# Head attention of a four-layer graph network: batches unrolled, weighted sums issued in pairs, a ring of six

## The reference

```python
q = (x @ W_q).reshape(Bn, Nn, NUM_HEADS, HEAD_DIM).transpose(0, 2, 1, 3)
...
scores = jnp.einsum('bhnd,bhmd->bhnm', q, k) / np.sqrt(HEAD_DIM).astype(np.float32)
adj = adjacency[None, None, :, :]
scores = jnp.where(adj == 0, -jnp.inf, scores)
attn = jax.nn.softmax(scores, axis=-1)
out = jnp.einsum('bhnm,bhmd->bhnd', attn, v)
```

## Time and profile before

| | us |
|---|---|
| median of 3 runs | 3907.07 |
| lowest and highest | 3902.5, 3911.31 |
| the profiled execution | 3912.55 |
| its span, first to last instruction | 3910.8 |
| first score of the head attention starts | 930.7 |
| its last pair of scores | 2873.0 |
| PE busy in the span | 3535.3 (90%) |
| VectorE busy in the span | 3162.2 (81%) |

### The profile page before, as it was taken

One profiled execution on the slowest core, in us unless ns is written; L12 is line 12 of the kernel. 1 busy time (PEld: TensorE's weight loads), 2 busy tenths in 40 slices (PEclk: granted clock), 3 DMA queues, 4 the chain that ended last, 5 costly groups with the idle time before them and its releaser, 6 DMA issues. The chain is left out here.

```text
span 3910.8 us, 71249 instructions
## 1 busy us (share of the span) xinstructions
PE 3535.3 (90%) x21228; PEld 1849.5 (47%) x21228; DVE 3162.2 (81%) x7145; ACT 1732.2 (44%) x3560; POOL 1820.8 (47%) x854
## 2 busy tenths in 40 slices
PE   5669999666999999999999999999968799789999
PEld 4669999441111111111111111111116599689999
DVE  6768888658999989999898998989967555367777
ACT  7811111552656656566565665656625423311100
POOL 2300000113888878888888887888843101100000
PEclk8779999886999999999999999999977799899999
DMA  6422121462100110001101010100125534221211
GB/s 238 168 100 82 50 87 50 154 232 104 27 19 14 29 27 27 21 12 29 27 27 26 8 27 27 27 23 11 28 90 210 199 144 155 101 91 68 82 65 45
DMA packets 66868, 288.66 MB, mean 74 GB/s; under 512 B 12483, under 2 KB 14917, under 8 KB 47045
## 3 DMA queue, kind: packets, MB, share of 16 engines
q1 hardware_dynamic: 64228, 267.55, 19.5%
q0 software_dynamic: 2304, 16.84, 1.0%
HBM read 174.12 MB, written 110.23 MB: 73 GB/s over the span
## 5 line engine op out<-in xcount | busy, mean ns | idle before, releaser
L1327 POOL TENSOR_TENSOR a_w<-a_w,keep_mask_t 128x1024 f32<-128x1024 f32 x768 | 1635.7, 2155 | 407.2 <-ACT a_w L1314 407.1
L1263 DVE CUSTOM_DVE_ANT_0 a_mx_ps<-a_mx_ps,a_mbias 128x512 f32<-128x512 f32 x2112 | 1389.4, 719 | 142.1 <-PE a_mx_ps L1189 129.6
L1314 ACT ACTIVATE a_w<-a_sc_ps 128x512 f32<-128x512 f32 x2048 | 1111.4, 595 | 812.3 <-PE a_sc_ps L1231 810.9
L1205 PE MATMUL a_o_ps<-a_w,a_v 128*33 128x512 f32 x4096 | 1083.6, 609 | 5.7 <-POOL a_w L1327 5.7
L839 PE MATMUL g_acc<-g_hv,g_w 128*128 128x129 f32 x8192 | 924.5, 276 | 36.4 <-ACT g_hv L797 24.8
L839 PEld LDWEIGHTS g_acc<-g_hv,g_w 128*128 128x128 f32 x8192 | 923.1, 193 | 38.1 <-DVE g_w L776 38.1
L776 DVE SCALAR_TENSOR_TENSOR g_w<-g_row,keep_s,keep_mask_t 128x1024 f32<-128x1024 f32 x512 | 647.2, 1282 | 203.7 <-PE g_acc L839 184.4
L1231 PE MATMUL a_sc_ps<-a_qs,a_ks 97*128 97x512 f16 x2048 | 634.4, 392 | 0.0
L1189 PEld LDWEIGHTS a_mx_ps<-a_ks,a_qs 32*128 32x128 f16 x2112 | 94.8, 91 | 893.9 <-DVE a_mx L1263 469.3
L1189 PE MATMUL a_mx_ps<-a_ks,a_qs 32*128 32x512 f16 x2112 | 411.3, 396 | 77.5 <-DVE a_mx L1263 33.4
L1276 DVE TENSOR_TENSOR a_w<-a_w,keep_mask_t 128x1024 f32<-128x1024 f32 x256 | 460.2, 1798 | 0.7
(11 more groups left out here) (178 smaller groups left out, 2278.2 us busy)
## 6 DMA issues: line engine op xcount, KB each, us to landing
p_x<-x SPq DMA_DIRECT2D x24, 1024.0 KB, 8.3
g_h<-h_nodes SPq DMA_DIRECT2D x16, 1032.0 KB, 6.2
p_adj_in<-in_adj SPq DMA_DIRECT2D x16, 1024.0 KB, 7.8
g_row<-u_rows SPq DMA_DIRECT2D x32, 512.0 KB, 7.3
a_v<-v SPq DMA_DIRECT2D x18, 528.0 KB, 3.6
a_ks<-k_hi SPq DMA_DIRECT2D x72, 128.0 KB, 2.8
a_qs<-q_hi SPq DMA_DIRECT2D x72, 128.0 KB, 3.0
v<-p_v SPq DMA_DIRECT2D x8, 1056.0 KB, 6.8
```

The source lines that it names most:

```text
L1205: mm = nc.tensor.matmul(o_ps[2 * HD * a:2 * HD * a + HD + 1, c % 2, :], v[u][:, jt, a, :], w[:, g % PB, a, :], start=(jt == 0), stop=(jt = ...
L1263: last = nc.vector.tensor_tensor_reduce(out=mx_ps[:, buf, a, :], in0=mx_ps[:, buf, a, :], in1=mbias[:, t, kc * BANK:(kc + 1) * BANK], scal ...
L1314: nc.scalar.activation(w[:, g % PB, a], sc_ps[:, n % SB], ACT.Exp, scale=SCALE).then_inc(exp_done, 1)
L1327: nc.gpsimd.tensor_tensor(w[:, g % PB], w[:, g % PB], keep["mask_t"][:, jt, c * BANK:(c + 1) * BANK].unsqueeze(1).to_broadcast([P, 2, BANK ...
```

## The change

`head_attention` alone is changed. All five loops over the batches become Python loops, so the instructions of the 1024 steps stand in line, and waits compare with constants. The ring `w` has six buffers, indexed by the step counted over all batches. TensorE issues in every even step the weighted sums of the two steps four and three back, over the borders of batches, and none in an odd step; the last four stand at the very end. The number of score buffers (`SB`), of max-product buffers (`MB`) and the waits of the scores are as before. ScalarE copies a batch's last chunk out behind exponential 3 of the next batch. SP stores it at the start of the next batch and loads the values of the second unit there. What had no reader is left out: the max products beyond the last chunk and the loads of batch 0 behind the last batch.

```diff
-    PB, LAG = 4, 3
+    PB, LAG = 6, 3
     SB, MB = 2, 2
...
+        def wanted(n, chunk):
...
+            return chunk < CHUNKS * B or chunk == CHUNKS * B and n in (-1, *range(TURN))
+
...
-            with sp.Fori(0, B) as b:
-                following = (b + 1) % B
+            for b in range(B):
+                more = b < B - 1
                 for c in range(CHUNKS):
-                    if c == CH:
+                    if c == CH and more:
                         sp.wait_ge(scored, 2 * (BODY * b + STEPS))
-                        load(sp, following, 0)
+                        load(sp, b + 1, 0)
                     if c >= 1:
                         store(b, c - 1)
-                    place_shift(sp, CHUNKS * b + c + 1, (c + 1) % CHUNKS // CH, (c + 1) % CH)
-                    if c == CH:
+                    elif b > 0:
+                        store(b - 1, CHUNKS - 1)
+                        sp.wait_ge(weighed, BODY * b + PB)
+                        load_v(sp, b, 1)
+                    if more or c < CHUNKS - 1:
+                        place_shift(sp, CHUNKS * b + c + 1, (c + 1) % CHUNKS // CH, (c + 1) % CH)
...
-                sp.wait_ge(scored, 2 * BODY * (b + 1))
-                load(sp, following, 1)
-                store(b, CHUNKS - 1)
-                sp.wait_ge(weighed, BODY * (b + 1) + PB)
-                load_v(sp, following, 1)
...
-            with pe.Fori(0, B) as i:
+            for i in range(B):
...
-                    if g >= LAG:
-                        weigh(g - LAG, i)
+                    if g % 2 == 0:
+                        for n in (BODY * i + g - 4, BODY * i + g - 3):
+                            if n >= 0:
+                                weigh(n % BODY, n // BODY)
                     for k in mine_now[1:]:
-                        slot(k, CHUNKS * i + g // T + 2, tu, tc)
-                for g in range(BODY - LAG, BODY):
-                    weigh(g, i)
+                        slot(k, chunk, tu, tc)
+            for g in range(BODY - 4, BODY):
+                weigh(g, B - 1)
...
-            with act.Fori(0, B) as i:
+            for i in range(B):
...
-                        nc.scalar.activation(w[:, g % PB, a], sc_ps[:, n % SB], ACT.Exp, scale=SCALE).then_inc(exp_done, 1)
+                        nc.scalar.activation(w[:, (BODY * i + g) % PB, a], sc_ps[:, n % SB], ACT.Exp, scale=SCALE).then_inc(exp_done, 1)
                     if g >= T + LAG and (g - LAG) % T == 0:
                         keep_rows((g - LAG) // T - 1, i)
-                keep_rows(2 * CH - 1, i)
+                    if g == LAG and i > 0:
+                        keep_rows(2 * CH - 1, i - 1)
+            keep_rows(2 * CH - 1, B - 1)
```

More of the change, by code:

```diff
@@ L1148, in store @@
                                  oe[2 * HD * a + HD:2 * HD * a + HD + 1, c % 2, :]).then_inc(o_stored[c % 2], 16)
-            with sp.Fori(0, B) as b:
-                following = (b + 1) % B
+            for b in range(B):
+                more = b < B - 1
                 for c in range(CHUNKS):
-                    if c == CH:
+                    if c == CH and more:
                         sp.wait_ge(scored, 2 * (BODY * b + STEPS))
-                        load(sp, following, 0)
+                        load(sp, b + 1, 0)
                     if c >= 1:
                         store(b, c - 1)
-                    place_shift(sp, CHUNKS * b + c + 1, (c + 1) % CHUNKS // CH, (c + 1) % CH)
-                    if c == CH:
-                        sp.wait_ge(weighed, BODY * b + STEPS + PB)
-                        load_v(sp, following, 0)
-                sp.wait_ge(scored, 2 * BODY * (b + 1))
-                load(sp, following, 1)
-                store(b, CHUNKS - 1)
-                sp.wait_ge(weighed, BODY * (b + 1) + PB)
-                load_v(sp, following, 1)
+                    elif b > 0:
[4 more added lines that the diff above has]
+                        place_shift(sp, CHUNKS * b + c + 1, (c + 1) % CHUNKS // CH, (c + 1) % CH)
+                    if c == CH and more:
+                        sp.wait_ge(weighed, BODY * b + STEPS + PB)
+                        load_v(sp, b + 1, 0)
+                if more:
+                    sp.wait_ge(scored, 2 * BODY * (b + 1))
+                    load(sp, b + 1, 1)
+            store(B - 1, CHUNKS - 1)
             for u in range(2):
-                sp.wait_ge(qk_loaded[u], LOADS * (B + 1))
-                sp.wait_ge(v_loaded[u], 16 * (B + 1))
                 sp.wait_ge(o_stored[u], 64 * CH * B)
-            sp.wait_ge(shift_placed, 32 * (CHUNKS * B + 1))
         @block.tensor
@@ L1177, in slot @@
                 n, buf = slots(first)[k], ring(k, c % 2)
-                if n < 0 and first:
+                if n < 0 and first or not wanted(n, chunk):
                     return
@@ L1220, in _ @@
                     on, tu, tc = target(g // T)
-                    if jt == 0 and tc == 0:
+                    chunk = CHUNKS * i + g // T + 2
+                    if jt == 0 and tc == 0 and chunk < CHUNKS * B:
                         pe.wait_ge(qk_loaded[tu], LOADS * (i + on + 1))
                     mine_now = of_step(jt)
-                    slot(mine_now[0], CHUNKS * i + g // T + 2, tu, tc)
+                    slot(mine_now[0], chunk, tu, tc)
                     if jt == 0:
@@ L1256, in slot @@
                 else:
-                    if not isinstance(due, int):
-                        dve.compute_val(due)
                     dve.wait_ge(*masks)
@@ L1313, in _ @@
                         act.wait_ge(scored, 2 * BODY * i + n + 1)
-                        nc.scalar.activation(w[:, g % PB, a], sc_ps[:, n % SB], ACT.Exp, scale=SCALE).then_inc(exp_done, 1)
+                        nc.scalar.activation(w[:, (BODY * i + g) % PB, a], sc_ps[:, n % SB], ACT.Exp, scale=SCALE).then_inc(exp_done, 1)
                     if g >= T + LAG and (g - LAG) % T == 0:
                         keep_rows((g - LAG) // T - 1, i)
-                keep_rows(2 * CH - 1, i)
+                    if g == LAG and i > 0:
+                        keep_rows(2 * CH - 1, i - 1)
+            keep_rows(2 * CH - 1, B - 1)
         @block.gpsimd
         def _(pool):
-            with pool.Fori(0, B) as i:
+            for i in range(B):
                 for g in range(BODY):
```

7 lines of the change are left out of this document (3 added, 4 removed).

## The result

| | median us | interval of the ratio to before |
|---|---|---|
| before | 3907.97 | |
| after | 4103.35 (4098.55 to 4104.41) | 1.0499 (1.0481 to 1.0517) |

The account below looks back on a forecast made before the run. Exponentials, uncovered by joining the weighted sums, were to bind each pair of steps. 64 chunks of 33.2 us, less 6 and 2.7, made 2116 against 1942: +174, so 4081 us, range 4030 to 4130.

Parts of the forecast that it names:

- The pair: Two head-attention steps on TensorE: 4.04 us against 3.68 now, the even step's second score waiting 0.48 us for an exponential.
- the joining's own pace of 3.56: TensorE's time for a pair of steps without the exponentials: 3.56 us, 0.12 saved by joining the weighted sums.
- The three terms behind the second score: To the first weighted sum 0.31 us, two sums and the way to the next max product 1.84, next scores 0.32.
- the start of the exponentials: On ScalarE, exponentials were taken to start 0.43 us after the scores, as in the steady step before.
- VectorE and the ring of products: Max products waiting for VectorE's reductions: hidden behind the exponentials' wait except once a chunk of 16 steps, making it 33.2 us.
- step 6: Its max product waits for the first of two VectorE reductions; its second score starts 0.44 us late, once a chunk.
- The borders: Between batches, drain and branch cost 6.7 us, seven times, 47 us; unrolling the loops removes them.
- The rule on weight loads: A Trainium skill rule: loads overlap matmuls only in differing row groups, giving a 4.19 us pair; the prediction followed the trace instead.
- VectorE costs more: Rival: VectorE masks and their overlap with GpSimd's add 1 us a chunk, +65, about 4145 us; chance 0.10.
- VectorE isn't in the way: Rival: reductions hold nothing, 32.5 us a chunk, -43, about 4038 us; chance 0.08.
- The boundary stays: Rival: straight code stalls TensorE at each batch as long as now, +47, about 4128 us; chance 0.05.
- The exponentials don't bind: Faster rival: the even step's second score isn't held by exponentials, about 3793 us, or 3844 at VectorE's present pace; chance 0.05.

Follow-up runs that it names:

- e2: The changed kernel with the two waits of a step's first exponential in the other order, so it carries the score's wait: 4080.2 us, ratio 1.0442.
- e3: The changed kernel with three score buffers instead of two, the bank taken from the weighted sums' second buffer: 3954.1 us, ratio 1.0120.
- e5: The changed kernel with exponentials of only 256 of 512 columns and masks that add instead of multiply: 3911.7 us, one run.
- e1: The kernel before with loops unrolled and the ring of six, but one weighted sum in each step as before: 3846.9 us, ratio 0.9845.
- e7: The changed kernel with three score buffers, and max products reduced over only 256 of 512 columns: 3875.3 us, one run.
- e4: The kernel before, loops kept, with only the joined weighted sums and a ring of six that starts anew each batch: 4141.4 us, ratio 1.0598.
- e6: The unrolled kernel with single weighted sums, with the old ring of four buffers instead of six: 3847.7 us, ratio 0.9850.

## Why the prediction was right

The forecast was 4081 in a range of 4030 to 4130, and 4103 was measured. Step by step:

- **The pair.** 1.08 + 2.96 = 4.04 was worked out from the start of a batch; after shows 1.14 + 2.97, e2 1.08 + 2.97. The cause is confirmed from two sides, by more buffers (e3) and by shorter exponentials (e5), and the joining's own pace of 3.56 is seen in e3. The three terms behind the second score (0.31, 1.84, 0.32) are 0.32, 1.85 and 0.32 in the rows of after.
- **The term that was mis-sized** is the start of the exponentials. The prediction took the steady 0.43 and said that the register instructions cost nothing. What it didn't see is that with them the form of the waits changes. Measured: 0.06 at each pair, 25.7 us of the stage (e2 against after), as much as the stage lies over the forecast (2141.8 against 2116). That the rest comes out even is partly luck: e2's chunk is 33.06 where I had 33.2, 9 us less in all. Against it stand some 7 us in e2's uneven chunks (0.7 at the start, 0.3 at each border, four chunks of 33.4 to 35.05) and 1.6 us of a slip in the sum: the interval left off at the end goes from an odd step to an even one and is 1.08, not 2.7.
- **VectorE and the ring of products.** The waits cover each other in all pairs but one of a chunk, as worked out: of the 1024 steps TensorE stands idle for VectorE in 62, once a chunk. At step 6 one is held (0.86 of idle [<-DVE] in the rows below), but the chunk's extra is smaller. I had 0.85 over eight pairs (0.21 for the double product, 0.44 at step 6, 0.2 at step 8); 33.47 less 8 x 4.11 is 0.59 (0.22, 0.37, nothing). At step 8 the product comes 0.67 behind the scores instead of 0.54, which the exponentials cover: the masks on VectorE took 1.24 on average, not up to 1.98.

```profile
1507.84 0.60 PE L1239 MATMUL a_sc_ps<-a_qs,a_ks 97*128 97x512 f16 x2
...
1509.30 0.39 PE L1196 MATMUL a_mx_ps<-a_ks,a_qs 32*128 32x512 f16 x2 [0.86 <-DVE a_mx L1271]
...
1509.62 0.60 PE L1239 MATMUL a_sc_ps<-a_qs,a_ks 97*128 97x512 f16 x2
```

- **The borders.** The term was too small, but the sum doesn't use it: it counts 64 equal chunks. 6.7 was read at the first border, which is one of the cheapest. From the last scores of a batch to the first of the next the seven borders took 8.5 to 9.7 (50 us over a step each, where 47 were expected), and the chunk behind each lost 0.4 to 2.0 more, 7 us in all. The prediction left out the clock there. Before, behind every border, after TensorE had idled for its branch, the granted clock stood at 1.2 GHz (0.50 of full speed) for 7 to 10 us, and a weighted sum took 1.92 instead of 1.05 (the row at 1179.42). In after and e1 the clock stays at 2.4 GHz over every border. How much of the 7 us is the clock was not taken apart. The first rows that the prediction borrowed for its pair reach into such a stretch (the product at 1174.84 takes 0.60, not 0.39). It did no harm, since ScalarE sets those two starts, and after shows the same ones at full clock.
- **The rule on weight loads** that the prediction cites. A sum behind a sum added 0.86 in after as before (1.91 for eight matmuls, 1.05 for four). The loads don't show, and e2's pair is 4.05, not the 4.19 that the rule would give; the row was the right guide.
- **The rivals.** "VectorE costs more" fell: VectorE had more idle time than before. "VectorE isn't in the way" (32.5 a chunk) fell by step 6: e2, whose exponentials start at the 0.43 of the sum, has 33.06. "The boundary stays" fell by e1 and by after's own border. "The exponentials don't bind" fell at the point that it named itself: the second score starts at s+1.62 in after and s+1.57 in e2. With it early (e3, e5) the loss mostly goes, but neither reaches the kernel before. Even with the exponentials out of the way, the held products and the step with the turned row cost more than the 0.12 a pair that joining saves. That part of the prediction's reasoning (a product held in every second pair) shows in full only in e3. And e7, with hardly a held product, has a chunk of 30.04 and 3875 us: it is under before only by the loops, and 28 us over e1, mostly at steps 4 to 6, behind the copy.

The two parts of the change pull apart: about -60 for the loops and +235 for the joining alone; together they are +195 rather than +175, of which the wait's form is 23 and came only with straight code (the exponentials start at 0.49 in e1 and after, at 0.43 in e4 and before). The fastest version is e1 (or e6): 3847 us, 1.5% under before and 6% under after.

## What to carry to other kernels

Before moving a covering piece of work, write down for each buffer of the ring how long its release takes from the start of the instruction that fills it, and what stands between that and the next use. With two score buffers that release is 1.57 us, and one weighted sum with its neighbours (1.84) just covers it; putting two sums in one place leaves 0.86 in the other. Saving a change of operand kind (0.12 a pair) is worth nothing against uncovering a wait four times as long. The trace of before may hold the new sequence somewhere, here at a loop's first steps, and its rows give the price without a run; look at the granted clock of those rows first.

## What the runs showed of the hardware

Of two waits ahead of an exponential, one goes into an instruction of its own, and a late signal that is waited for there reaches the exponential 0.06 us later than one that the exponential carries itself (0.49 against 0.43 behind the scores; after and e2). The wait that is met last belongs with the instruction.

The masks on VectorE took 1.80 us on average while TensorE kept an even rhythm (before and e1), and 1.24 in the joined order; the stage's total for them fell by 143 us (460.2 before, 317.3 after).

The traces show where the difference comes from. Wherever a mask on VectorE started with more than 0.25 us left of a running mask on GpSimd, it ended 1.08 us after GpSimd's did, however much had been left (192 masks in before, 191 in e1, 250 in e7, with a spread of 0.002 us); with less than 0.15 us left it took 1.22 in before and after. It goes the other way too: in e5 a mask on GpSimd took 2.7 where VectorE's had 0.5 to 0.9 us to run at its start, and 2.13 where none was running. So two such masks with their operands in SBUF didn't share the time in these runs: nearly all of the second waited for the end of the first. In the joined order GpSimd was mostly at its end or still idle when VectorE started.

It brought nothing, since VectorE wasn't what TensorE waited for. It shows that an engine's busy time can fall while the kernel becomes slower.

Of TensorE's clock: before and in e4 it was granted at 1.2 GHz for 7 to 14 us behind each of the seven borders, and in e1 over the whole stage behind 939 us, and in after but for 3.4 us at 2114, at 2.4 GHz. After's waits of half a microsecond in each pair, with TensorE busy 90% (242.00 of 268 us), did not lower it.
